# A running sum of gamma times v kept in SBUF, in place of a carry copied from tile to tile in PSUM

## The chip, the cores and the metric

The kernel runs on one core of one Trainium2 chip. The metric is the device time of one execution in microseconds. Before the change the median of three runs is 630.31 us (630.24 to 630.64).

## What is computed

The input x is 4 batches of 2048 tokens with 256 features, in float32. An attention layer without softmax is followed by a layer of softly routed experts; each is added to its input and normalised. The part that matters here is the attention:

```python
q, k, v = mlp_q(x), mlp_k(x), mlp_v(x)        # gelu(x @ W1 + b1) @ W2 + b2
scores = einsum('bid,bjd->bij', q, k) / scale
scores = scores * tril(ones((T, T)))          # causal, no softmax
out = einsum('bij,bjd->bid', scores, v)
out = layernorm(out) * ln_w + ln_b
x = layernorm(x + out)
```

There is no softmax, so the part of `out` that comes from earlier tiles is the product of a query with a running state (the sum of k transposed times v). The bias of q adds to each score a number that depends on the key token alone. The kernel calls it gamma: column 256 of `k_tok`. For a tile of 128 tokens, all earlier tiles therefore add two things: h of q times the state, and one row, the same for all 128 tokens, which is the sum of gamma times v over all earlier tokens.

## The kernel before the change, in words

64 tiles of 128 tokens stand in 16 groups of four; a batch is 16 tiles, four groups. Each engine runs its own program, a `body` for each group, called by `run_groups`. The body of group g projects group g (`project`) and attends for group a = g - 1 (`attend`); `ja` is the place of group a in its batch (0 to 3), i that of a tile in its batch (0 to 15) and c that of a tile in its group. Body 0 only projects. Body 15 (`more=False`) also begins the expert stage: it scales the first tokens and takes their norms. After it comes a last body that only attends, `last_chunks` on TensorE. The expert stage begins behind a barrier of all engines.

Products are made in three passes of a reduced type (`fp32r`): each operand is split into a rounded part (`_hi`, made by ScalarE) and a remainder (`_lo`, made by VectorE or GpSimd), and `split3` issues hi times hi, hi times lo and lo times hi.

TensorE's order in a body is: hidden layer of k (two jobs), scores of group a, hidden layer of q (two jobs), `chunk` 0, first job of v's hidden layer, `chunk` 1, second job of v's hidden layer, two tiles of k's projection, `chunk` 2, two more tiles of k's projection, `chunk` 3, first half of v's projection, transposes of k, second half of v's projection. A `chunk` holds, for one tile, the masked scores times v (`attend_chunk`, 3 matmuls), the queries times the state (`read_state`, 6), the update of the state in PSUM (`update_state`, 6), and the `carry` (3). The state is rounded by ScalarE (`round_state`) and split by VectorE (`split_state`) before the next tile reads it.

The row of gamma times v lives in the output tile in PSUM itself. `carry` of tile i adds gamma (broadcast over the 128 columns of the weights) times v of tile i into the output tile of i + 1, on top of the row that ScalarE had copied there from the output tile of i (`preload`, PSUM to PSUM). Gamma has its own rounding on ScalarE (in `round_ktok`) and its own split on VectorE (`split_gamma`). Two wide matmuls at the start (`mark_out`) set the output banks up, so that nothing later needs a starting matmul.

GpSimd's order in a body: `add_ln_b(g)` (adds ln_b to the loaded x), `split_hv(g, 0)`, `invert_o(a, 0)`, `split_hv(g, 1)`, `split_x(g + 1)`, `split_ktok(g, 0)`, `invert_o(a, 1)`, `split_ktok(g, 1)`, two `split_v`, `invert_z(a)`, `invert_x1(a)`. In body 15 `add_beta(0)` stands in place of `split_x`. VectorE's order: splits of k's hidden layer around `mask_scores`, `split_masked`, both splits of q's hidden layer, then `follow(0)` (the split of the state behind tile 0), statistics and outputs of tiles 0 and 1, biases of k and v, and at the end `split_gamma`, `z_statistics` and `z_deviation`. In body 15 `scale_tokens(0)` stands between the two splits of q's hidden layer and `scale_tokens(1)` behind `bias_k`. In body 0 VectorE ends with `mu_factors`, which waits for GpSimd's `invert_mu_norms`; TensorE's `spread_mu_factors` in body 1 waits for that.

The SP queue loads x transposed and x, one after the other, for each group: the first behind `x_split`, the second behind `xb_ready`, which `add_ln_b` signals.

## Time and profile before

| | before |
|---|---|
| median of 3 runs | 630.31 us |
| the profiled execution, its own time | 629.76 us |
| its span | 628.0 us |
| TensorE (PE) busy | 606.5 us, 97% |
| VectorE (DVE) busy | 432.7 us, 69% |
| ScalarE (ACT) busy | 414.8 us, 66% |
| GpSimd (POOL) busy | 349.8 us, 56% |
| mean granted clock of TensorE | 0.995 |

The span is what lies between the first and the last instruction; 1.76 us of the execution lie around it. The attention takes about the first 416 us, the expert stage the rest. Matmuls overlap, so the length shown for one (280 ns for 256 columns) is longer than the distance from its start to the next one's; a cost is read from the distance between starts.

### The profile page before, as it was taken

The page shows a single profiled execution, that of the slowest core. Times are in us where ns is not written, and L with a number is a line of the kernel's source. Part 1 is how long each engine was busy: PE and PEld are TensorE (multiplying, and loading weights), DVE is VectorE, ACT ScalarE, POOL GpSimd, SP SyncE. Part 2 cuts the span into 40 slices and gives each one's busy share as a digit, 9 for nine tenths or more (in the row PEclk, how much of TensorE's full clock was granted, in tenths as well). Part 3 has the DMA queues.
Part 4 walks back from the last instruction along what each step waited for, and adds up shares of the span by engine and source line. Part 5 has one row for each costly group of instructions (what it writes and reads, how often), then busy time and mean ns, then how long its engine had stood idle before and what let it go on. Part 6 is the DMA issues. An engine that isn't in the chain of part 4 may idle for free. (4 is left out here: it accounts for less than half of the span.)

```text
span 628.0 us, 12369 instructions
## 1 busy us (share of the span) xinstructions
PE 606.5 (97%) x4100; PEld 557.8 (89%) x4100; DVE 432.7 (69%) x943; ACT 414.8 (66%) x921; POOL 349.8 (56%) x359
## 2 busy tenths in 40 slices
PE   7999999999999999999999999999999999979994
PEld 5889999989999999899998998989999999868883
DVE  5587677677676776777767768886656554437784
ACT  4756767767677667676676776766766666334765
POOL 2937567676675675766766757665344333104443
PEclk9999999999999999999999999999999999999997
DMA  8311211111012012111120110030000000032444
GB/s 224 105 35 33 69 34 34 49 53 35 33 33 67 33 33 67 33 33 33 34 67 33 33 35 1 2 68 2 1 1 0 0 0 2 2 67 69 166 142 160
DMA packets 29310, 30.21 MB, mean 48 GB/s; under 512 B 5310, under 2 KB 25180, under 8 KB 29276
## 3 DMA queue, kind: packets, MB, share of 16 engines
q1 hardware_dynamic: 29264, 29.78, 15.9%
q8 instruction: 18, 0.29, 0.2%
q14 instruction: 16, 0.13, 0.1%
q10 hardware_dynamic: 12, 0.00, 0.0%
HBM read 21.39 MB, written 8.39 MB: 47 GB/s over the span
## 5 line engine op out<-in xcount | busy, mean ns | idle before, releaser
L563 ACT ACTIVATE h_hi<-bank,bias_col 128x512 fp32r<-128x512 f32 x96 | 66.4, 692 | 35.1 <-PE bank L690 31.7
L488 POOL TENSOR_TENSOR h_lo<-xn_all,h_hi 128x512 fp32r<-128x512 f32 x32 | 41.4, 1294 | 71.1 <-ACT xn_all L565 71.0
L688 PE MATMUL bank<-xnT_hi,w_hi 128*128 128x512 f32 x188 | 76.0, 404 | 0.0
L689 PE MATMUL bank<-xnT_lo,w_hi 128*128 128x512 f32 x188 | 74.2, 395 | 0.0
L690 PE MATMUL bank<-xnT_hi,w_lo 128*128 128x512 f32 x188 | 74.2, 395 | 0.0
L1067 DVE TENSOR_TENSOR state_lo<-bank,state_hi 128x512 fp32r<-128x512 f32 x57 | 39.1, 686 | 43.4 <-ACT state_hi L604 43.4
L1442 PE MATMUL bank<-xn_all,e_tok 128*128 128x257 f32 x256 | 66.4, 382 | 0.2
L1348 ACT ACTIVATE e_tok<-bank,shift,xinv 128x256 f32<-128x256 f32 x64 | 36.1, 565 | 44.9 <-PE bank L1425 24.0
L1522 DVE COPY ET_all<-bank 128x256 f32<-128x256 f32 (+1 forms) x64 | 27.0, 424 | 53.1 <-PE bank L1436 52.7
L494 POOL TENSOR_TENSOR ktok_lo<-xn_all,ktok_hi 128x512 fp32r<-128x512 f32 x32 | 38.1, 1192 | 44.3 <-ACT ktok_hi L580 44.3
L604 ACT CAST state_hi<-bank 128x512 fp32r<-128x512 f32 x57 | 33.5, 588 | 41.7 <-PE bank L830 41.5
L1514 PE MATMUL bank<-w_sb,ET_all 128*128 128x256 f32 x256 | 55.5, 379 | 0.8 <-ACT w_sb L1387 0.8
L1514 PEld LDWEIGHTS bank<-w_sb,ET_all 128*128 128x128 f32 x256 | 48.6, 190 | 7.6 <-ACT w_sb L1387 1.1
L483 POOL TENSOR_TENSOR x_all<-x_all,lnb_rows 128x512 f32 (+1 forms) x32 | 47.2, 1494 | 11.6 <-DMA x_all<-in_L_attn_x 11.6
L219 POOL TENSOR_TENSOR xn_all<-xn_all,b_rows 128x1024 f32<-128x1024 f32 x16 | 35.0, 2187 | 26.7 <-DVE xn_all L212 26.7
L1423 PE MATMUL bank<-mu_hi,xnT_hi 128*128 128x256 f32 x128 | 47.2, 369 | 0.8 <-POOL blank L1303 0.8
L1442 PEld LDWEIGHTS bank<-xn_all,e_tok 128*128 128x128 f32 x256 | 43.6, 190 | 4.3 <-ACT slot_inT L1370 0.9
L690 PEld LDWEIGHTS bank<-xnT_hi,w_lo 128*128 128x128 f32 x188 | 35.4, 188 | 8.6
L1011 DVE TENSOR_TENSOR h_lo<-hq,h_hi 128x512 fp32r<-128x512 f32 x32 | 32.4, 1016 | 13.9 <-ACT hq L565 13.9
L500 POOL TENSOR_TENSOR v_lo<-xn_all,v_hi 128x512 fp32r<-128x512 f32 x32 | 40.7, 1290 | 0.3 <-ACT v_hi L595 0.3
L689 PEld LDWEIGHTS bank<-xnT_lo,w_hi 128*128 128x128 f32 x188 | 35.5, 189 | 5.8
L688 PEld LDWEIGHTS bank<-xnT_hi,w_hi 128*128 128x128 f32 x188 | 35.4, 188 | 5.8
(188 smaller groups left out, 2072.0 us busy)
## 6 DMA issues: line engine op xcount, KB each, us to landing
x_all<-in_L_attn_x SPq DMA_DIRECT2D x16, 512.0 KB, 3.5
out<-xn_all SPq DMA_DIRECT2D x16, 512.0 KB, 3.0
xn_all<-in_xT SPq DMA_DIRECT2D x15, 512.0 KB, 3.7
w_sb<-in_L_ffn_w SPq DMA_DIRECT2D x2, 512.0 KB, 5.4
xn_all<-in_L_ffn_w SPq DMA_DIRECT2D x2, 512.0 KB, 6.3
xn_all<-in_xT SPq DMA_DIRECT2D x2, 256.0 KB, 3.6
x_all<-in_L_attn_W2k SPq DMA_DIRECT2D x1, 258.0 KB, 4.4
x_all<-in_L_attn_W2q SPq DMA_DIRECT2D x1, 258.0 KB, 5.4
```

The costliest lines, as they stand in the source:

```text
L483: pool.tensor_tensor(xp, xp, lnb_rows[:, :].unsqueeze(1).to_broadcast([P, 2, D]), ALU.add).then_inc(xb_ready, 1)
L488: pool.tensor_tensor(h_lo[:, V_SLOT, m, :], hv[:, m, :], h_hi[:, V_SLOT, m, :].bitcast(F32), ALU.subtract).then_inc(hv_split, 1)
L494: pool.tensor_tensor(ktok_lo[:, pair, :], k_tok[:, pair, 0:D], ktok_hi[:, pair, :].bitcast(F32), ALU.subtract).then_inc(ktok_split, 1)
L500: pool.tensor_tensor(v_lo[:, pair, :], v_tok[:, pair, :], v_hi[:, pair, :].bitcast(F32), ALU.subtract).then_inc(v_split, 1)
L563: nc.scalar.activation(h_hi[:, h_slot(j, n), m, :], ps, ACT.Gelu, bias=bias(n, m))
L688: nc.tensor.matmul(ps, w[0], xs[0], start=start, stop=False, skip_group_check=shared)
L689: nc.tensor.matmul(ps, w[0], xs[1], start=False, stop=False, skip_group_check=shared)
L690: return nc.tensor.matmul(ps, w[1], xs[0], start=False, stop=stop, skip_group_check=shared)
L1067: nc.vector.tensor_tensor(lo[:, :, :], state_halves, hi[:, :, :].bitcast(F32), ALU.subtract).then_inc(state_split, 1)
L1423: nc.tensor.matmul(ps, hi, mu_hi[:, kb, :], start=(kb == 0), stop=False)
L1442: last = nc.tensor.matmul(fold_ps[s][:, 0:D + 1], e_tok[:, t % 4, s * P:(s + 1) * P], xn[q][:, t % GT, :], start=(t == 0), stop=(t == TB - 1))
L1514: last = nc.tensor.matmul(mix_ps[k % 2][t][:, 0:D], ET_all[:, s, toks], so[:, k // GB, s, :], start=(s == 0), stop=(s == SB - 1))
```

## The change

- `carry` of tile c now adds the whole row at once: the 128 x 128 matrix of ones times a tile `v_sum`, whose row p is the sum over all earlier tiles of gamma times v at place p. It has two passes, ones times the rounded part and ones times the remainder. It stands inside `chunk`, behind the first of the two products, and the first product of a tile now starts the accumulation. Tile 0 of a batch has no carry.
- `v_sum` has four slots. VectorE fills them: `sum_v(c)` writes slot c + 1 from slot c, `close_sum` writes slot 0 for the next group. ScalarE rounds them in two pairs (`round_vsum`), GpSimd splits them in two pairs (`split_vsum`).
- The rounding and split of gamma, the copies `preload` and their waits are gone. Tiles 0 and 2 of a group now wait for `z_ready` on TensorE itself.
- VectorE: `follow(0)` stands ahead of the split of the second half of q's hidden layer.
- GpSimd: `add_ln_b(g)` goes from the head of the body to behind `split_x(g + 1)`; in body 15 it stands ahead of `add_beta(0)`.
- `causal` has one 128 x 128 block, not four.

```diff
 # GpSimd
-                pool.memset(causal[:, :, :], 1.0)
+                pool.memset(causal[:, :], 1.0)
...
+                def split_vsum(g, m):
+                    pool.wait_ge(vsum_rounded, 2 * g + m + 1)
+                    pair = slice(2 * m, 2 * m + 2)
+                    pool.tensor_tensor(vsum_lo[:, pair, :], v_sum[:, pair, :], vsum_hi[:, pair, :].bitcast(F32),
+                                       ALU.subtract).then_inc(vsum_split, 1)
...
+                    if attend and project:
+                        split_vsum(a, 0)
                     if project:
-                        add_ln_b(g)
                         split_hv(g, 0)
                     if attend:
                         invert_o(pool, a, 0)
                     if project:
+                        if attend:
+                            split_vsum(a, 1)
                         split_hv(g, 1)
                         if more:
                             split_x(g + 1)
-                        else:
+                        add_ln_b(g)
+                        if not more:
                             add_beta(pool, 0, 0)
                         split_ktok(g, 0)
...
                         split_v(g, 1)
+                        if not more:
+                            split_vsum(g, 0)
+                            split_vsum(g, 1)
                     if attend and project:
                         invert_z(pool, a, (j - 1) % 2)
 # ScalarE
-                    nc.scalar.copy(gam_hi[:, :], k_tok[:, :, D]).then_inc(gam_rounded, 1)
...
-                def preload(ba, i):
-                    act.wait_ge(carried, CB * ba + i - 1)
-                    act.wait_ge(z_ready, TB * ba + i + 2 - i % 2)
-                    nc.scalar.copy(out_tile(i % GT), out_tile((i - 1) % GT)).then_inc(preloaded, 1)
+                def round_vsum(g, m):
+                    act.wait_ge(v_summed, GT * g + 2 * m + 1)
+                    pair = slice(2 * m, 2 * m + 2)
+                    nc.scalar.copy(vsum_hi[:, pair, :], v_sum[:, pair, :]).then_inc(vsum_rounded, 1)
...
                     hidden(g, j, WK1, 0)
+                    if attend:
+                        round_vsum(a, 0)
                     hidden(g, j, WK1, 1)
...
                     if attend:
                         follow(0)
+                    if attend:
+                        round_vsum(a, 1)
                     hidden(g, j, WV1, 0)
...
                     round_v(g, 0)
                     if not more:
+                        round_vsum(g, 0)
                         norms(act, 0, 0, range(GT))
                     round_v(g, 1)
+                    if not more:
+                        round_vsum(g, 1)
 # TensorE
-                def carry(a, ba, i):
-                    c = i % GT
-                    if c == 0:
-                        pe.wait_ge(gam_split, a + 1)
-                    if i > 0:
-                        pe.wait_ge(preloaded, PB * ba + i)
-                    split3(out_tile((i + 1) % GT),
-                           (gam_hi[:, c:c + 1].to_broadcast([P, P]), gam_lo[:, c:c + 1].to_broadcast([P, P])),
-                           (v_hi[:, c, :], v_lo[:, c, :]), False, False, shared=True).then_inc(carried, 1)
+                def carry(a, c, start):
+                    pe.wait_ge(vsum_split, 2 * a + c // 2 + 1)
+                    if isinstance(a, int) and a == 0 and c == 1:
+                        pe.wait_ge(ones_rounded, 1)
+                    nc.tensor.matmul(out_tile(c), ones_r[:, :], vsum_hi[:, c, :], start=start, stop=False,
+                                     skip_group_check=True)
+                    nc.tensor.matmul(out_tile(c), ones_r[:, :], vsum_lo[:, c, :], start=False, stop=False,
+                                     skip_group_check=True)
 
                 def chunk(a, ja, ba, c, p):
                     i = GT * ja + c
-                    if 0 < i < TB - 1:
-                        pe.wait_ge(preloaded, PB * ba + i)
+                    if c % 2 == 0:
+                        pe.wait_ge(z_ready, GT * a + c + 2)
                     if i == 0:
-                        pe.wait_ge(z_ready, GT * a + 2)
                         last = attend_chunk(a, c, True, True)
                     elif c == 0:
-                        read_state(ba, i, c, p, False)
+                        read_state(ba, i, c, p, True, False)
+                        carry(a, c, False)
                         last = attend_chunk(a, c, False, True)
                     else:
-                        attend_chunk(a, c, False, False)
-                        last = read_state(ba, i, c, p, True)
+                        attend_chunk(a, c, True, False)
+                        carry(a, c, False)
+                        last = read_state(ba, i, c, p, False, True)
                     last.then_inc(chunk_done, 1)
                     if i < TB - 1:
                         update_state(a, c, i == 0)
-                        carry(a, ba, i)
...
                     def read(c):
-                        if c < GT - 1:
-                            pe.wait_ge(preloaded, PB * ba + i + c)
-                        read_state(ba, i + c, c, p, False, tail_hi[c], tail_lo[c])
+                        if c % 2 == 0:
+                            pe.wait_ge(z_ready, GT * a + c + 2)
+                        carry(a, c, c % 2 == 0)
+                        read_state(ba, i + c, c, p, False, False, tail_hi[c], tail_lo[c])
 # VectorE
+                def sum_v(g, j, c):
+                    dve.wait_ge(v_biased, 2 * g + c // 2 + 1)
+                    if not (isinstance(g, int) and g == 0):
+                        dve.wait_ge(v_summed, GT * g + c)
+                        dve.wait_ge(vsum_split, 2 * g)
+                    elif c > 0:
+                        dve.wait_ge(v_summed, c)
+                    gamma = k_tok[:, c, D:D + 1]
+                    if j == 0 and c == 0:
+                        last = nc.vector.tensor_scalar(v_sum[:, 1, :], v_tok[:, 0, :], gamma, None, ALU.mult)
+                    else:
+                        last = nc.vector.scalar_tensor_tensor(out=v_sum[:, c + 1, :], in0=v_tok[:, c, :], scalar=gamma,
+                                                              in1=v_sum[:, c, :], op0=ALU.mult, op1=ALU.add)
+                    last.then_inc(v_summed, 2 if j == GB - 1 and c == GT - 2 else 1)
+
+                def close_sum(g, j):
+                    if j < GB - 1:
+                        dve.wait_ge(v_summed, GT * g + GT - 1)
+                        dve.wait_ge(vsum_split, 2 * g + 1)
+                        nc.vector.scalar_tensor_tensor(out=v_sum[:, 0, :], in0=v_tok[:, GT - 1, :],
+                                                       scalar=k_tok[:, GT - 1, D:D + 1], in1=v_sum[:, GT - 1, :],
+                                                       op0=ALU.mult, op1=ALU.add).then_inc(v_summed, 1)
...
+                    if attend:
+                        sum_v(a, ja, 1)
+                        sum_v(a, ja, 2)
                     split_h(g, j, WQ1, 0)
                     if not attend:
                         split_m()
                     if not more:
                         scale_tokens(0, 0)
+                    if attend:
+                        follow(0)
+                        close_sum(a, ja)
                     split_h(g, j, WQ1, 1)
                     if attend:
-                        follow(0)
...
-                    split_gamma(g)
+                    sum_v(g, j, 0)
+                    if not more:
+                        sum_v(g, j, 1)
+                        sum_v(g, j, 2)
                     if attend:
                         z_statistics(a, p, 1)
...
                 split_first_x()
                 dve.wait_ge(masks_ready, 1)
+                nc.vector.tensor_copy(ones_r[:, :], ones[:, :]).then_inc(ones_rounded, 1)
                 spread_b2k()
```

## Rows read from the trace of the kernel before

**Rows 1.** Engines by stretch: length; busy us (instructions) by engine; TensorE's clock; DMA.

```profile
270.00:300.00 30.00, 30.00 (x222) 28.38 (x222) 20.66 (x42) 21.42 (x42) 19.39 (x19) 1.00 0.14 41
...
620.00:628.00 8.00, 0.00 (x0) 0.00 (x0) 1.03 (x3) 3.43 (x7) 1.13 (x2) 0.57 0.41 148
```

**Rows 2.** Waits of TensorE: us in total, times, longest.

```profile
PE bank L688 <- DVE state_lo L1067: 1.5, 4, 1.0
```

**Rows 3.** Groups of TensorE instructions: one of carry's three passes; busy us, mean ns.

```profile
L688 PE MATMUL bank<-v_hi,gam_hi 128*128 128x256 f32 x60 | 16.7, 279 | 0.0
```

**Rows 4.** Timeline, TensorE, a group with ja = 1: start us, length us.

```profile
152.69 0.39 PE L688 MATMUL bank<-xnT_hi,w_hi 128*128 128x512 f32 x1
...
160.81 0.28 PE L688 MATMUL bank<-v_hi,masked_hi 128*128 128x256 f32 x1
...
161.88 0.28 PE L688 MATMUL bank<-v_hi,gam_hi 128*128 128x256 f32 x1
...
162.23 0.40 PE L688 MATMUL bank<-xnT_hi,w_hi 128*128 128x512 f32 x1
```

**Rows 5.** Timeline, TensorE: tile 1's reads of the state that waited (ja = 0; body 15).

```profile
138.62 0.39 PE L688 MATMUL bank<-state_hi,h_hi 128*128 128x256 f32 x1 [0.17 <-DVE state_lo L1067]
...
390.22 0.38 PE L688 MATMUL bank<-state_hi,h_hi 128*128 128x256 f32 x1 [1.01 <-DVE state_lo L1067]
```

**Rows 6.** Groups by line: instructions with the shapes of the added ones.

```profile
L595 ACT CAST v_hi<-xn_all 128x512 fp32r<-128x512 f32 x32 | 19.9, 623 | 14.7 <-DVE xn_all L1047 14.7
L212 DVE SCALAR_TENSOR_TENSOR xn_all<-x_all,r_all,g_rows 128x256 f32<-128x256 f32 x64 | 26.6, 479 | 0.0
L500 POOL TENSOR_TENSOR v_lo<-xn_all,v_hi 128x512 fp32r<-128x512 f32 x32 | 40.7, 1290 | 0.3 <-ACT v_hi L595 0.3
```

**Rows 7.** Timeline, GpSimd: its part beside VectorE's instructions of rows 8.

```profile
127.86 2.58 POOL L500 TENSOR_TENSOR v_lo<-xn_all,v_hi 128x512 fp32r<-128x512 f32 x2
...
153.59 2.54 POOL L500 TENSOR_TENSOR v_lo<-xn_all,v_hi 128x512 fp32r<-128x512 f32 x2
...
158.32 1.01 POOL L204 TENSOR_TENSOR r_all<-ve_x,minus_half 128x4 f32 x1 [0.17 <-POOL ve_x L202]
159.29 3.00 POOL L483 TENSOR_TENSOR x_all<-x_all,lnb_rows 128x512 f32 x2
...
384.27 2.55 POOL L483 TENSOR_TENSOR x_all<-x_all,lnb_rows 128x512 f32<-128x512 f32 x2
```

**Rows 8.** Timeline, VectorE: instructions with two inputs in SBUF.

```profile
129.32 1.13 DVE L1040 TENSOR_TENSOR gam_lo<-xn_all,gam_hi 128x4 fp32r<-128x4 f32 x1
...
154.57 0.34 DVE L1040 TENSOR_TENSOR gam_lo<-xn_all,gam_hi 128x4 fp32r<-128x4 f32 x1
...
161.60 1.24 DVE L1011 TENSOR_TENSOR h_lo<-hq,h_hi 128x512 fp32r<-128x512 f32 x1 [0.46 <-ACT hq L565]
```

**Rows 9.** Timeline, GpSimd and TensorE, body 0 to body 1.

```profile
28.44 0.71 POOL L535 TENSOR_TENSOR mu_inv<-mu_n,minus_half 128x2 f32<-128x2 f32 x1
...
31.95 0.71 PE L916 MATMUL bank<-mu_diag,ones 128*128 128x128 f32 x4 [0.81 <-DVE mu_diag L1086]
```

**Rows 10.** Timeline, body 15 and the last body, all engines.

```profile
396.29 2.21 POOL L219 TENSOR_TENSOR xn_all<-xn_all,b_rows 128x1024 f32<-128x1024 f32 x1
...
399.42 1.67 DVE L212 SCALAR_TENSOR_TENSOR xn_all<-x_all,r_all,g_rows 128x256 f32<-128x256 f32 x4
...
404.43 0.42 ACT L226 ACTIVATE square<-xn_all 128x256 f32<-128x256 f32 x1
...
406.04 0.60 ACT L595 CAST v_hi<-xn_all 128x512 fp32r<-128x512 f32 x1
...
408.19 1.01 POOL L193 TENSOR_TENSOR r_z<-ve_z,minus_half 128x4 f32<-128x4 f32 x1 [0.18 <-DVE ve_z L175]
...
408.91 0.39 PE L830 MATMUL bank<-v_hi,ktok_hi 128*128 128x256 f32 x1 [0.16 <-DVE h_lo L1067]
...
415.33 0.28 PE L690 MATMUL bank<-v_hi,masked_lo 128*128 128x256 f32 x1
```

More of the change, by code:

```diff
@@ L283, in build @@
             ku_rows = asb("ku_rows", [P, KC])
-            gam_hi = asb("gam_hi", [P, GT], F32R)
-            gam_lo = asb("gam_lo", [P, GT], F32R)
+            v_sum = asb("v_sum", [P, GT, D])
+            vsum_hi = asb("vsum_hi", [P, GT, D], F32R)
+            vsum_lo = asb("vsum_lo", [P, GT, D], F32R)
+            ones_r = asb("ones_r", [P, P], F32R)
             bias_rows = asb("bias_rows", [3 * KB, P])
@@ L289, in build @@
             lnb_rows = asb("lnb_rows", [P, D])
-            causal = asb("causal", [P, GT, P])
+            causal = asb("causal", [P, P])
             xT_hi, xT_lo = xnT_hi[0], xnT_lo[0]
@@ L466, in _ @@
                                    base=0, pattern=[[-1, P]], channel_multiplier=1)
-                pool.affine_select(out=causal[:, :, :], in_=causal[:, :, :], compare_op=ALU.is_ge, fill=0.0,
-                                   base=0, pattern=[[0, GT], [1, P]], channel_multiplier=-1).then_inc(masks_ready, 1)
+                pool.affine_select(out=causal[:, :], in_=causal[:, :], compare_op=ALU.is_ge, fill=0.0,
+                                   base=0, pattern=[[1, P]], channel_multiplier=-1).then_inc(masks_ready, 1)
                 def split_x(g):
@@ L630, in body @@
                         round_masked(a)
-                        preload(ba, i + 3)
                         apply_z(act, a - 1, (ja - 1) % 2, (0, 1))
@@ L752, in fold_weights, with warm_up @@
                     last.then_inc(ku_done, 1)
-                def mark_out():
+                def warm_up():
                     for ps in out_ps:
-                        last = nc.tensor.matmul(ps[:, :], ident[:, :], causal[:, :, :].rearrange("p c n -> p (c n)"),
-                                                start=True, stop=True)
-                    last.then_inc(out_marked, 1)
+                        nc.tensor.matmul(ps[:, :], ident[:, :], causal[:, :].unsqueeze(1).to_broadcast([P, GT, P]),
+                                         start=True, stop=True)
                 def project_k(g, j, t):
@@ L804, in scores, with read_state @@
                         last.then_inc(scores_done, 1)
-                def read_state(ba, i, c, p, stop, hi=state_hi, lo=state_lo):
+                def read_state(ba, i, c, p, start, stop, hi=state_hi, lo=state_lo):
                     pe.wait_ge(state_split, CB * ba + i)
@@ L812, in read_state @@
                         last = split3(out_tile(c), (h_hi[:, p, kb, toks], h_lo[:, p, kb, toks]),
-                                      (hi[:, kb, :], lo[:, kb, :]), False, stop and kb == KB - 1, shared=True)
+                                      (hi[:, kb, :], lo[:, kb, :]), start and kb == 0, stop and kb == KB - 1, shared=True)
                     return last
```

23 lines of the change are left out of this document (7 added, 16 removed).

## The prediction

> **What bounds the kernel.** I read the engines by stretch first. In any full stretch of the attention TensorE is busy for all of it at clock 1.00, while VectorE has 69% and GpSimd 65% [rows 1]. Then TensorE's own waits: on another engine inside the attention's loop there is one entry, VectorE's split of the state, 1.5 us in four waits [rows 2]. So the loop is TensorE's, and matmuls taken out of it come off the time one for one, as long as nothing new ends late. The parts where TensorE isn't the bound are body 0 to body 1 and body 15 to the barrier; there chains over the other engines decide.
>
> **1. Fewer passes.** Before, 60 carries of three passes [rows 3]. Three passes take the step from 161.88 to 162.23 us, 0.35 us, so 0.117 us each [rows 4]. After, tiles 1 to 15 of each batch have two: 120. Outside `last_chunks` it is 171 against 112 (57 carries times 3; 56 times 2), 59 fewer: 59 x 0.117 = **-6.9 us**. That is all TensorE can give. I take no gain in `last_chunks`, which waits for other engines (5). The ScalarE copies `preload` go too; no wait of TensorE names them [rows 2], so they are worth nothing.
>
> **2. The state's split ahead of q's second.** Tile 1 reads the state behind VectorE. With ja = 0 that read began 0.17 us late by the row and about 0.32 by the distance of starts, and the next one 0.1 late: 0.42 us, in three batches. In body 15 it was 1.01 us late, some 1.27 in all, since `scale_tokens(0)` and q's second split (0.6 us) stood ahead [rows 5]. With ja = 0 the split now comes some 0.1 us before the need: -1.3. In body 15 I find 0.25 us of stall left (two `sum_v` are new ahead of it, q's second split is gone): -1.0. Together **-2.3 us** (-1.3 to -2.5).
>
> **3. The new wait: tile 0's carry.** With ja = 1, 2, 3 TensorE wants it right behind `read_state`, where the masked product stood: 8.12 us after the body's start (160.81 - 152.69) [rows 4]. Queued behind it are the whole body's matmuls. The chain that must be done: `sum_v(0)` on VectorE (0.48 us), `round_vsum(0)` on ScalarE (0.62), `split_vsum(0)` on GpSimd (1.29) [rows 6]. GpSimd gets to it only behind `invert_x1`, whose last instruction is followed by `add_ln_b` at 159.29 [rows 7]. ScalarE has been done for 3 us by then.
> What shifts 159.29? Rows 8 beside rows 7: VectorE's 4-column split of gamma took 1.13 us from 129.32 and ended when GpSimd's `split_v` did (130.44); from 154.57 it took 0.34 and ended about where the first `split_v` did. GpSimd in turn took 3.00 us for two `add_ln_b` with VectorE's 512-column split in between, 2.55 alone [rows 7, 8]. So an instruction of VectorE with two inputs in SBUF and one of GpSimd exclude each other, and 512 columns cost GpSimd 0.45 us. `sum_v(0)` has 256 columns and falls between the two `split_v`: +0.22. Then 159.51 + 1.29 + 0.05 = 160.85 against 160.81. It is a knife's edge; with a restart I take 0.1 us in each of 11 bodies (12 with ja > 0, less the last): **+1.1 us**. Bounds: 0, and 0.6 each, 6.6 us, if `sum_v(1)` (wanted at 159.88) gets in first.
> The Trainium skill, in "SBUF — State Buffer", section "SBUF: two separate sides", calls the pair shared by VectorE and GpSimd an exclusive lock held for the whole instruction, also against VectorE instructions with two SBUF inputs. Rows 7 and 8 agree for `tensor_tensor`; no row here has the form of `sum_v` against a long GpSimd instruction. Without the lock 3 would be 0 us and 5 would be 4.2 us.
>
> **4. Start and body 1.** The smaller `causal` lets TensorE start 0.6 us sooner, of which 0.4 is left behind the biases. But `add_ln_b(0)` (2.55 us) now stands ahead of `split_ktok(0)`, where GpSimd had no idle time; before, it came at the start and covered GpSimd's wait for h of v. So `mu_inv` (28.44) ends 2.1 us later even with the earlier start, and behind it `split_vsum` (1.29) starts at once, so `mu_factors` on VectorE is locked out until 32.6. `mu_diag` is ready at 33.2 and TensorE's product with it, which began at 31.95 after 0.81 us idle, begins at 33.2 [rows 9]: +1.3. VectorE is busy without a gap to tile 1's read and has two more `sum_v`: +0.3. **+1.6 us** (0 to 2.2).
> In the other bodies the moved `add_ln_b` falls in GpSimd's idle 3.2 us ahead of `split_ktok`, with 0.4 us to spare; if that went, `split_ktok` would be late by as much, and TensorE wants it 10 us later. Its DMA: x of the next group is queued some 13 us later and still has a body's 24 us until it is used; the next load of transposed x waits behind it by 3 us, with a body to spare. Nothing. `split_vsum(1)` fits in GpSimd's idle 1.4 us ahead of `split_hv(1)` and ends 0.25 us before tile 2's carry. `sum_v(1)`, `sum_v(2)` and `close_sum` fall in VectorE's idle time around q's splits. `z_ready` is a body old. Nothing each.
>
> **5. The end, body 15 and behind.** Here each edit hits a full engine [rows 10].
> - GpSimd: `add_ln_b(15)` (2.55 us) stands ahead of `add_beta(0)`, which moves from 396.3 to 398.9 and ends at 401.1. VectorE's `scale_tokens(1)` (two inputs in SBUF) wants to begin at 399.42 and is locked out: 1.7 us, and VectorE has no gap behind it. Perhaps `split_ktok` gets in between for another 1.2.
> - ScalarE: `round_vsum(15, 0)` stands ahead of the norms (404.43) and needs `sum_v(0)`, which VectorE reaches at the place of the old gamma split, 406.1, without the lock-out. So ScalarE stands idle, then does the norms (1.6 us), then `round_v(1)`, which began at 406.04: at 409.0 without lock-outs, 409.9 to 411.2 with them. Then a second `round_vsum` (0.52), the rounding of the turned tokens, the rounding of the state behind tile 12.
> - TensorE's update at 408.91 waits for that and comes at 412.5, 413.4 or 414.7.
> - GpSimd has two `split_vsum` (2.55) and the late `split_v` ahead of `invert_z` (408.19, then 414 to 415.6). VectorE's `shift_z` waits for it, and the next state split is queued behind `shift_z`.
> Followed on, the last matmul (415.33, and the barrier) comes 4.2 us later without the lock, 4.9 with it, 6.0 if `split_ktok` gets in. I take **+5.4 us** (3.4, ScalarE's chain alone, to 6.5).
>
> **Sum.** -6.9 - 2.3 + 1.1 + 1.6 + 5.4 = **-1.1 us**. It is made against the profiled execution (629.76 us: span 628.0 and 1.76 around it), 0.55 us below the median; the change goes on the median: 630.31 - 1.1 = **629.2 us**. A difference under 0.2% (1.3 us) can't be told from none here, so the forecast lies just inside "the same".
>
> **Rivals.**
> - A, the ends are covered. If ScalarE's and GpSimd's queues at the end bend less (5 at its low bound, 3.4), body 1 costs nothing and the first carry is never late, the sum is -6.9 - 2.3 + 3.4 = -5.8: **624.5 us**. For it: 5 is a chain of ten steps, each a place to be wrong. Against: `round_vsum(15, 0)` ahead of the norms waits for the end of VectorE's queue whatever else happens.
> - B, slower: tile 0's carry waits 0.5 us in each of the 11 bodies, since `sum_v(1)` or a later `invert_x1` pushes `split_vsum(0)` out. 4.4 us more than forecast, **633.6 us**. It decides from a lateness of 0.2 us more: at 0.3 us a body (3.3 us in place of 1.1) the kernel is slower. For it: the margin is -0.04 us. Against: the lateness doesn't add up, since a TensorE that waits gives the chain its time back.
> - C, the clock. Where TensorE did nothing for the 8 us of the last stretch, the granted clock was 0.57 [rows 1], so it was at the lower level (1.2 GHz) for most of it. The end now has a stall of some 4 us. If the clock falls there, the 4.6 us of matmuls behind it take up to twice as long, part of it hidden by their waits: +2.3, **631.5 us**. Against: before, no stretch inside the attention is below 1.00.
> The Trainium skill, "TensorE: Matmul & The Clock Gate", section "What's actually happening", says that idleness takes the clock to the lower level and activity gives it back. Last stretch and loop agree with both levels; no row of before has a stall of 4 us inside the work.
>
> **How the numbers follow.** Forecast 0.50, A 0.22, B 0.16, C 0.12. The forecast's own range is 627.4 to 630.9. Faster by over 0.2% (under 629.05): A's 0.22 and 0.21 of the forecast, 0.43. Within 0.2%: 0.26 of the forecast, 0.02 of B, 0.06 of C, 0.34. Slower: 0.03, 0.14 and 0.06, 0.23. Range 625.8 to 632.2: past the forecast's own on both sides, with most of C, half of A and the near part of B; the rest is under 2 in 10.
>
> **What would show it.** (1) Two passes a carry, 120 in all, 0.117 us apart. (2) No wait of TensorE on the state's split with ja = 0, at most 0.3 us in body 15. (3) TensorE waits on GpSimd's `vsum_lo`, about 11 times, 0 to 0.2 us; GpSimd's `split_vsum(0)` ends within 0.2 us of the carry's start. `sum_v(0)` begins when a `split_v` ends. (4) TensorE's product with `mu_diag` begins near 33.2 us with over 2 us idle. (5) ScalarE idle some 3 us ahead of the norms in body 15, TensorE's second update in `last_chunks` some 4 to 6 us after where it stood, counted from the end of v's projection, and the barrier 4.9 to 6 later. I am wrong if the barrier moves by under 3 us, if the carry waits over 0.3 us a body, or if the expert stage, which has no edit, takes another time.

## The result and the profile after

The changed kernel takes 635.28 us (median, 634.27 to 635.80) against 630.41 for the kernel before beside it: ratio 1.0075, 95% interval 1.0058 to 1.0093. Measured again later it is 1.0070 (1.0055 to 1.0086). By these ratios it is slower by 4.4 to 4.7 us; forecast was 1.1 us faster, and the range ended at 632.2. Even the fastest of its ten executions, 632.74 us, lies above that.

The first profiled execution took 635.80 us (span 634.1; before 629.76 and 628.0). I set TensorE's marks side by side: the first transposition of k in each body, the first matmul of the expert stage, and the last.

| stretch | before | after | difference | forecast |
|---|---|---|---|---|
| start to k's turn in body 0 | 22.73 | 24.41 | +1.7 | -0.4 |
| body 1 | 27.77 | 29.85 | +2.1 | +1.3 |
| bodies 2 to 14 | 324.99 | 320.62 | -4.4 | -6.0 |
| body 15 | 26.51 | 25.98 | -0.5 | -1.4 |
| k's turn in body 15 to the experts | 14.45 | 21.40 | +7.0 | +5.4 |
| expert stage | 202.00 | 202.31 | +0.3 | 0 |

(Forecast: the terms of the prediction laid on these stretches; body 1 is 2.0 less six passes.) The loop gave less than thought, and both ends took more. First the carry, groups of TensorE's instructions, answering to [rows 3]: busy, mean ns, idle time ahead.

```profile
L852 PE MATMUL bank<-vsum_hi,ones_r 128*128 128x256 f32 x60 | 17.5, 291 | 0.1
L854 PE MATMUL bank<-vsum_lo,ones_r 128*128 128x256 f32 x60 | 17.1, 285 | 0.0
```

There are 120 passes, and TensorE's idle time ahead of the carries is 0.1 us in all. GpSimd's `split_vsum(0)` and TensorE's carry in a group with ja = 1 (timeline) show how near it is:

```profile
161.78 1.30 POOL L506 TENSOR_TENSOR vsum_lo<-v_sum,vsum_hi 128x512 fp32r<-128x512 f32 x1
...
163.19 0.32 PE L852 MATMUL bank<-vsum_hi,ones_r 128*128 128x256 f32 x1
163.35 0.28 PE L854 MATMUL bank<-vsum_lo,ones_r 128*128 128x256 f32 x1
```

The split ends 0.1 us ahead of the use; the prediction had it 0.04 us behind. Next TensorE's waits, answering to [rows 2]:

```profile
PE bank L843 <- DVE h_lo L1099: 4.3, 1, 4.3
...
PE bank L927 <- DVE mu_diag L1118: 2.3, 1, 2.3
...
PE bank L244 <- DVE xn_all L1054: 1.2, 1, 1.2
...
PE bank L715 <- ACT bias_col L632: 0.7, 1, 0.7
```

The waits for `state_lo` are gone from the top of this list (one of 0.4 us is left, in body 15); four waits at the two ends stand there. Engines by stretch; the number behind POOL's is TensorE's granted clock, which was 1.00 in the same stretches before:

```profile
35.00:38.00 3.00, 2.89 (x9) 2.50 (x10) 2.93 (x9) 0.59 (x1) 0.00 (x0) 0.50 0.00 0
...
411.00:413.00 2.00, 0.00 (x0) 0.00 (x0) 1.56 (x2) 1.98 (x4) 2.00 (x3) 1.00 0.00 0
414.00:417.00 3.00, 3.00 (x16) 3.00 (x16) 2.26 (x7) 2.06 (x4) 3.00 (x3) 0.50 0.00 0
```

Behind the 2.27 us without work in body 1, and behind the 4.34 us in `last_chunks`, the clock stands at its lower level, 1.2 GHz: 9 matmuls in 3 us of body 1, 20 in the same stretch before. The first hidden matmuls are slow too (timeline, TensorE, the last line from the kernel before):

```profile
6.02 0.27 PE L911 MATMUL bank<-ident,bias_rows 6*128 6x6 f32 x1
7.02 2.07 PE L715 MATMUL bank<-xnT_hi,w_hi 128*128 128x512 f32 x4 [0.73 <-ACT bias_col L632]
8.89 1.91 PE L719 MATMUL bank<-xnT_hi,w_lo 128*128 128x512 f32 x4
```

```profile
8.22 1.10 PE L705 MATMUL bank<-xnT_hi,w_lo 128*128 128x512 f32 x4
```

Four took 1.91 us, 1.10 before. This is not a fall of the clock but a late rise. The trace's first record of the clock, at the full level, begins at some 11.1 us of the span here and at some 6.7 us in the trace of before. Ahead of it there is no record (the view then prints 1.00), and the rate of the matmuls is what shows the lower level; it goes up where that record begins.

Body 1, answering to [rows 9] (timelines of three engines):

```profile
32.56 0.71 POOL L548 TENSOR_TENSOR mu_inv<-mu_n,minus_half 128x2 f32<-128x2 f32 x1
33.25 1.26 POOL L506 TENSOR_TENSOR vsum_lo<-v_sum,vsum_hi 128x512 fp32r<-128x512 f32 x1
...
33.31 1.22 DVE L1114 TENSOR_SCALAR mu_fac<-mu_inv,scale_col 128x2 f32<-128x2 f32 x1 [4.32 <-POOL mu_inv L548]
...
35.11 1.22 PE L927 MATMUL bank<-mu_diag,ones 128*128 128x128 f32 x4 [2.27 <-DVE mu_diag L1118]
```

`mu_fac` begins 0.06 us behind `split_vsum` and ends with it. The end, answering to [rows 10]:

```profile
397.82 2.20 POOL L219 TENSOR_TENSOR xn_all<-xn_all,b_rows 128x1024 f32<-128x1024 f32 x1
...
398.64 3.79 DVE L212 SCALAR_TENSOR_TENSOR xn_all<-x_all,r_all,g_rows 128x256 f32<-128x256 f32 x4
...
400.82 1.33 POOL L494 TENSOR_TENSOR ktok_lo<-xn_all,ktok_hi 128x512 fp32r<-128x512 f32 x1 [0.79 <-ACT ktok_hi L592]
...
407.33 0.62 ACT L601 CAST vsum_hi<-v_sum 128x512 fp32r<-128x512 f32 x1 [2.24 <-DVE v_sum L1071]
407.85 0.41 ACT L226 ACTIVATE square<-xn_all 128x256 f32<-128x256 f32 x1
...
409.46 0.60 ACT L606 CAST v_hi<-xn_all 128x512 fp32r<-128x512 f32 x1
...
413.30 0.39 PE L843 MATMUL bank<-v_hi,ktok_hi 128*128 128x256 f32 x1 [4.34 <-DVE h_lo L1099]
...
421.45 0.28 PE L704 MATMUL bank<-v_hi,masked_lo 128*128 128x256 f32 x1
```

This is the forecast chain, link by link: `scale_tokens(1)` locked out, `split_ktok` in between, ScalarE idle ahead of the norms, then `round_v(1)` and TensorE's update. The forecast's times are on the clock of the kernel before, where k's turn in body 15 came 1.1 us later (402.00, here 400.86). Brought to that clock `round_v(1)` is at 410.6 (forecast 409.9 to 411.2 with lock-outs) and the update at 414.4 (412.5 to 414.7). What the forecast leaves out is the matmuls behind.

The expert stage, which has no edit, takes 0.3 us more; that was one of the prediction's signs of being wrong. In this profile the clock falls there too, for 3.4 us from 557.2, and in that of before it doesn't. But in the trace of `before_state_first` it falls there as well, and that stage is within 0.1 us of before's. So the clock doesn't explain it, and the cause stays open.

### The profile page after: what moved, and what is told of

Same layout as the page of the kernel before. It is cut to its first block and busy times, and to the rows that moved or that the text cites. A ratio compares the mean times of both kernels' runs of the same rounds, so it can differ in the third digit from the quotient of the medians.

```text
span 634.1 us, 12270 instructions
## 1 busy us (share of the span) xinstructions
PE 608.6 (96%) x4040; PEld 559.4 (88%) x4040; DVE 449.0 (71%) x989; ACT 412.8 (65%) x881; POOL 384.9 (61%) x391
## 5 line engine op out<-in xcount | busy, mean ns | idle before, releaser
L500 POOL TENSOR_TENSOR v_lo<-xn_all,v_hi 128x512 fp32r<-128x512 f32 x32 | 42.8, 1362 | 3.1 <-ACT v_hi L606 3.1
L236 POOL TENSOR_TENSOR xinv<-n_low,minus_half 128x4 f32<-128x4 f32 x16 | 16.3, 1016 | 42.6 <-DVE n_low L231 42.6
L506 POOL TENSOR_TENSOR vsum_lo<-v_sum,vsum_hi 128x512 fp32r<-128x512 f32 x32 | 41.2, 1289 | 0.0
```

Of the source, the lines that this page charges most:

```text
L500: pool.tensor_tensor(v_lo[:, pair, :], v_tok[:, pair, :], v_hi[:, pair, :].bitcast(F32), ALU.subtract).then_inc(v_split, 1)
L506: pool.tensor_tensor(vsum_lo[:, pair, :], v_sum[:, pair, :], vsum_hi[:, pair, :].bitcast(F32), ALU.subtract).then_inc(vsum_split, 1)
```

## The experiments

Differences in us are (ratio - 1) x 630.3.

**The addresses.** In the loop the matmuls of the projections followed each other more slowly than before, though nothing in them was changed. The changed kernel's larger tensors move h and all behind it by 11,232 bytes.

```diff
             gam_lo = asb("gam_lo", [P, GT], F32R)
+            pad = asb("pad", [P, 2808])
```

> The kernel before with one unused tensor of 11,232 bytes per partition ahead of h_hi, so that h_hi, h_lo, v_hi, ktok_hi, state_hi and all behind them lie at the addresses that they have in the changed kernel; no instruction differs. Question: in the changed kernel the matmuls of the projections follow each other more slowly than before (the time from m_hi by h_hi to m_lo by h_hi 126 ns against 118, from w_lo by h_hi to w_hi by h_lo 120 against 117), some 0.14 us a body, about 2 us in all. Theory ADDRESS: it is the place of these tensors in SBUF; this kernel then takes 632.4 us (631.5 to 633), and its trace has the spacings of the changed kernel. Rival TRAFFIC: it is the other engines' new work on SBUF (sum_v, round_vsum, split_vsum) beside the matmuls; then this kernel is the kernel before, 630.4 us within 0.3, with spacings of 118 and 117. Chances 0.6 and 0.4.

Ratio 1.0025 (1.0016 to 1.0034): +1.6 us with not one instruction changed. Groups of TensorE in 75 to 375 us, first of the kernel before, then of this one:

```profile
L690 PE MATMUL bank<-w_hi,h_lo 128*128 128x256 f32 x97 | 27.0, 279 | 0.0
L688 PE MATMUL bank<-m_hi,h_hi 128*128 128x258 f32 x96 | 27.0, 281 | 0.0
```

```profile
L689 PE MATMUL bank<-m_hi,h_hi 128*128 128x258 f32 x96 | 27.2, 284 | 0.0
...
L691 PE MATMUL bank<-w_hi,h_lo 128*128 128x256 f32 x96 | 27.0, 282 | 0.0
```

These two groups take 3 ns more each. Of the six groups on `h_hi` and `h_lo` in this stretch five are longer, by 1 to 4 ns, and one (`m_hi,h_lo`) is not; those on the state are not longer. Marks of bodies 2 to 14 (first transposition of k), before:

```profile
50.50 1.04 PE L788 MATMUL bank<-ident,xn_all 128*128 128x128 f32 x8
...
375.49 1.04 PE L788 MATMUL bank<-ident,xn_all 128*128 128x128 f32 x8
```

and with the padding:

```profile
51.20 1.04 PE L789 MATMUL bank<-ident,xn_all 128*128 128x128 f32 x8
...
377.56 1.04 PE L789 MATMUL bank<-ident,xn_all 128*128 128x128 f32 x8
```

326.36 against 324.99: +1.4 us of these 13 bodies. The theory ADDRESS holds, with a little less than the 2 us that it expected; the traffic of the other engines isn't needed for most of it.

```diff
             ones_r = asb("ones_r", [P, P], F32R)
+            pad = asb("pad", [P, 8])
```

> The changed kernel with one unused tensor of 32 bytes per partition ahead of bias_rows, so that h_hi and all behind it lie 11,264 bytes (11 times 1,024) behind where they lay before, in place of 11,232. Theory ADDRESS with an alignment of up to 1,024 bytes: the spacings of the projections go back to 118 and 117 ns, some 2 us less, 633.3 us (632.5 to 634.2). ADDRESS without a role of this alignment, or TRAFFIC: 635.3 us within 0.8. The stalls and the clock at the start, in body 1 and at the end are not touched.

Ratio 1.0081 (1.0063 to 1.0098), no gain; bodies 2 to 14 take 320.42 us (320.62). A distance of 11 times 1,024 bytes doesn't restore the pace, so alignment of up to 1,024 isn't what decides.

```diff
-            v_sum = asb("v_sum", [P, GT, D])
-            vsum_hi = asb("vsum_hi", [P, GT, D], F32R)
-            vsum_lo = asb("vsum_lo", [P, GT, D], F32R)
             ones_r = asb("ones_r", [P, P], F32R)
+            ones = asb("ones", [P, P])
+            b1_row = asb("b1_row", [PAIRS, P])
+            pad = asb("pad", [P, 8])
...
             b2_row = asb("b2_row", [E, D])
+            v_sum = asb("v_sum", [P, GT, D])
+            vsum_hi = asb("vsum_hi", [P, GT, D], F32R)
+            vsum_lo = asb("vsum_lo", [P, GT, D], F32R)
```

> The changed kernel with v_sum, vsum_hi and vsum_lo laid behind all other tensors of the attention, and ones, b1_row and 32 unused bytes in the gap, so that h_hi, h_lo and all up to mu_diag lie at the addresses of the kernel before; no instruction differs. The kernel before with these tensors at the changed kernel's addresses took 1.6 us more. Theory ADDRESS ALONE: the changed kernel gets back what the other lost, 1.6 us, ratio to before 1.0050, and w_lo by h_hi to w_hi by h_lo takes 117 ns again (120). Theory ADDRESS AND TRAFFIC: half of it, 0.5 to 1.0 us. Rival: any new place costs, since other tensors now meet each other: under 0.4 us. Chances 0.5, 0.25, 0.25.

Ratio 1.0051 (1.0033 to 1.0068), 1.2 to 1.5 us under the two measurements of the changed kernel, though the intervals overlap; bodies 2 to 14 take 319.51 us, 1.1 less. So most comes back. Which pair of tensors meets where stays open.

**The start.**

```diff
                                         ).then_inc(bias_turned, 1)
+                    nc.tensor.matmul(out_ps[0][:, 0:3 * P], ident[:, :],
+                                     causal[:, :].unsqueeze(1).to_broadcast([P, 3, P]), start=True, stop=True)
```

> The changed kernel with one more matmul of 384 columns on ident and causal behind the transposition of the biases, into a bank that is overwritten later; it fills the 0.73 us in which TensorE had nothing to do from 6.29 to 7.02 us. Theory CLOCK AT THE START: the changed kernel's first hidden matmuls ran at half rate (4.72 us for twelve of 512 columns, 2.91 before) because TensorE was idle just behind the warm-up; with the gap filled they take 2.9 to 3.3 us, the fold begins at 10.0 to 10.4 us (11.74 without, 10.09 before), and the whole is 1.4 us shorter: 633.9 us. Rival: it is the earlier begin of the warm-up (2.31 us, 2.99 before) that counts, and the clock rises no sooner whatever fills the gap: 635.3 us or 0.1 more, the fold at 11.7. A second rival: the two kernels' rates at the start differ from one execution to the next, and one profile doesn't tell; then the time moves by under 0.5 us. Chances 0.5, 0.25, 0.25.

Ratio 1.0073 (1.0060 to 1.0086): no gain in the median, though in its profile the first four hidden matmuls take 1.39 us and the fold (the matmuls on `x_all` behind them) begins at 10.05 us, as forecast by the first theory. The second rival has to be taken too. Of eight profiles of the changed kernel and its edits without the filling, five have the half rate: the fold begins at 11.3 to 12.1 us, and the first record of the full clock at some 10.6 to 11.9. Three have not (fold at 9.4 to 10.6, record at 5.4 to 6.8). The warm-up begins at 2.31 us in all eight. TensorE's idle time behind it is 0.3 to 0.9 us in the five and 0.6 to 1.4 us in the three, so neither the earlier begin nor the length of the gap decides by itself. Both profiles with the filling have the full rate (record at 6.3 and 6.8), and so have the four of the kernel before and its edits (6.2 to 8.5; in the padded one it comes within the first hidden matmuls). Where the rate is full, k's turn in body 0 comes at 22.5 to 23.3 us with the change, by and large where it was (22.73); where it is half, at 24.0 to 24.8: +1.7 us in the first profile. That the filling prevents it is suggested by two profiles and not shown by the times.

**Body 1.**

```diff
                     if project:
+                        if not attend:
+                            add_ln_b(g)
                         split_hv(g, 0)
...
-                        add_ln_b(g)
+                        if attend:
+                            add_ln_b(g)
```

> The changed kernel with add_ln_b(0), and it alone, back at the head of GpSimd's body 0. My step 4: mu_inv (32.56 us in the changed kernel) comes some 2.5 us sooner, near 30.1, since GpSimd covers its wait for h of v again; mu_fac is no longer locked out by split_vsum; TensorE's product with mu_diag, which began at 35.11 after 2.27 us without work, begins near 33.4 with 0.3 to 0.9 us without. Theory STALL AND CLOCK: with a stall that short the granted clock stays 1.00 in 34 to 38 us (0.50 for 3.4 us of it in the changed kernel, price some 1.7 us), so the gain is 1.5 + 1.6 = 3.1 us: 632.2 us (631.5 to 633). Rival STALL ALONE (the clock falls all the same, or it fell in the profiled execution alone): 1.5 us, 633.8 us. Rival: the stall has another cause (VectorE's sum_v in body 1): under 0.5 us.

Ratio 1.0032 (1.0021 to 1.0043): 2.4 to 2.7 us less, outside the intervals of the changed kernel. Timelines of GpSimd and VectorE, and the stretch of the clock row:

```profile
30.48 0.71 POOL L551 TENSOR_TENSOR mu_inv<-mu_n,minus_half 128x2 f32<-128x2 f32 x1
31.94 1.28 POOL L506 TENSOR_TENSOR vsum_lo<-v_sum,vsum_hi 128x512 fp32r<-128x512 f32 x1 [0.74 <-ACT vsum_hi L604]
```

```profile
31.23 0.23 DVE L1117 TENSOR_SCALAR mu_fac<-mu_inv,scale_col 128x2 f32<-128x2 f32 x1 [0.69 <-POOL mu_inv L551]
```

```profile
35.00:38.00 3.00, 3.00 (x18) 2.42 (x17) 2.80 (x5) 2.77 (x6) 0.00 (x0) 1.00 0.00 0
```

Without GpSimd beside it `mu_fac` takes 0.23 us, not 1.22; TensorE doesn't wait there, and the clock stays. Body 1 takes 26.35 us: 3.5 less than with the change, 1.4 less than before it. My price for the fall (1.7) was too high: two profiles (of end_queues and third_pass below) have the same 2.27 us stall and no fall, and their body 1 is 0.8 to 1.0 us shorter (29.03, and 29.25 less three added passes of 0.117, against 29.85); that the waits behind take in the rest is likely and not shown.

**The moves alone, on the kernel before.**

```diff
                     if attend:
                         follow(0)
+                    split_h(g, j, WQ1, 1)
```

(VectorE; `split_h` stood ahead of `follow(0)`.)

> The kernel before with one edit of the change alone: VectorE splits the state behind tile 0 ahead of q's second split. My step 2: TensorE's waits for that split (1.5 us in four) and the launches behind them, 0.42 us in each of three batches and 1.0 in body 15, go: 2.3 us less, ratio 0.9964. Rival: q's second split, 0.6 us later, now lets tile 1 or the scores of the next group wait; then the gain is under 1 us. Rival: in body 15 the gain is given back where v_hi is waited for: 1.3 us.

Ratio 0.9969 (0.9957 to 0.9981): -2.0 us, forecast -2.3. Bodies 2 to 14 give 1.25 us (forecast 1.3), body 15 0.6 (1.0): the read there still waits 0.41 us.

```diff
                     if project:
-                        add_ln_b(g)
                         split_hv(g, 0)
...
                             split_x(g + 1)
+                        add_ln_b(g)
```

> The kernel before with one edit of the change alone: GpSimd's add_ln_b behind the splits of h of v and of x, in every body. Body 1: mu_inv would come some 2.5 us later (28.44 to 30.9), but with add_ln_b(1) gone from behind it mu_fac is not locked out (1.23 us before) and no split_vsum stands there, so TensorE's product with mu_diag comes near 31.9 as before: 0 us (0 to 0.8). Body 15: add_ln_b(15) and add_beta(0) lie on scale_tokens(1), which takes 3.8 us in place of 1.67; v's biases, and all behind them, come 1.2 us later at TensorE: 1.2 to 2.1 us. Sum 1.5 us, ratio 1.0024. Theory that the move costs by itself what the whole change loses in body 1 (3 us with the clock): ratio 1.006 or more. Rival, it costs nothing alone: ratio 1.0000 within 0.0008.

Ratio 0.9981 (0.9971 to 0.9991): -1.2 us where I expected +1.5. The missed effect: `add_ln_b` at the head of a body locked VectorE's `split_h` of q out (1.24 us in [rows 8], 0.69 in this run), and the state's split behind it came late for that. With it moved, the waits go in the loop (1.25 us, the same ones as in the run above, so the two don't add) and body 15 is 1.2 us shorter. The price at the end is 0.6 us, not 1.2 to 2.1, with `scale_tokens(1)` at

```profile
397.52 3.03 DVE L212 SCALAR_TENSOR_TENSOR xn_all<-x_all,r_all,g_rows 128x256 f32<-128x256 f32 x4
```

and body 1 loses 0.5 us (1.30 us stall at `mu_diag`, 0.81 before, no fall of the clock).

**The end.** First the order of two queues:

```diff
                     if not more:
-                        round_vsum(g, 0)
                         norms(act, 0, 0, range(GT))
                     round_v(g, 1)
                     if not more:
+                        round_vsum(g, 0)
                         round_vsum(g, 1)
...
                         split_v(g, 1)
-                        if not more:
-                            split_vsum(g, 0)
-                            split_vsum(g, 1)
                     if attend and project:
                         invert_z(pool, a, (j - 1) % 2)
+                        if not more:
+                            split_vsum(g, 0)
+                            split_vsum(g, 1)
```

> The changed kernel with two orders altered in body 15: on ScalarE the norms and round_v(1) come ahead of both round_vsum(15); on GpSimd invert_z comes ahead of both split_vsum(15). My step 5, ScalarE's share: without the wait for sum_v(0) (2.24 us idle) the norms begin at 404.9 and round_v(1) at 406.6 in place of 409.46; then the rounding of the second vsum waits for sum_v(2) at 408.6, so the turned tokens are rounded at 409.1 (410.49) and TensorE's second update of last_chunks comes near 411.3 in place of 413.30. The gain is 2.0 us if the clock falls all the same in the stall of 2.3 us that is left, 3.7 if it doesn't: 633.3 or 631.6 us, ratio to before 1.0043 or 1.0016. Rival: GpSimd and VectorE are the bound there, and the barrier moves by under 1 us.

Ratio 1.0055 (1.0039 to 1.0070), and not from the end: from k's turn in body 15 to the experts it takes 21.49 us (21.40); this profile has no fall in body 1. ScalarE, VectorE, TensorE (timelines):

```profile
408.76 0.62 ACT L601 CAST vsum_hi<-v_sum 128x512 fp32r<-128x512 f32 x1 [1.62 <-DVE v_sum L1071]
```

```profile
405.88 2.16 DVE L1071 SCALAR_TENSOR_TENSOR v_sum<-xn_all,v_sum 128x256 f32<-128x256 f32 x2
```

```profile
411.62 0.58 PE L843 MATMUL bank<-v_hi,ktok_hi 128*128 128x256 f32 x1 [3.47 <-DVE h_lo L1099]
```

`round_v(1)` comes early, and GpSimd's `split_v(1)` with it, which now locks out `sum_v` (2.16 us for two, 1.18 in the change). ScalarE waits for the last `sum_v` in place of the first. The stall is 3.47 us and the clock falls behind it again.

```diff
                     if project:
+                        if not more:
+                            add_ln_b(g)
                         split_hv(g, 0)
```

> The same, and add_ln_b(15) back ahead of split_hv(15, 0), so that add_beta(0) and split_ktok no longer lie on scale_tokens(1). My step 5, the lock-out's share: scale_tokens(1) takes 1.67 us in place of 3.79, v's biases and the turning of the tokens come 1.2 us sooner (TensorE's idle 1.16 us ahead of it goes), and the end gains 1.2 to 2.1 us over the run before it: ratio to before 1.0005 to 1.0025. Rival: the last body's own chain (state splits behind each other on VectorE, two more split_vsum on GpSimd) hides it; under 0.5 us.

Ratio 1.0081 (1.0049 to 1.0113): no gain, and the interval overlaps with that of the run before it. The end is shorter, 18.68 us in place of 21.49, but body 15 is 2.2 us longer (28.23 against 25.99). `add_ln_b(15)`, behind `split_vsum` now, lies on q's split (1.78 us, 0.69 in the run before it). The scaling of tokens comes later for that and runs beside `split_hv` (2.70 us in place of 1.67), and the state's split stands behind it. Waits of TensorE:

```profile
PE bank L846 <- DVE h_lo L1102: 3.4, 1, 3.4
PE bank L705 <- DVE state_lo L1102: 3.0, 1, 3.0
```

Neither order helped. So the next edit takes the work out of these queues.

```diff
-                        carry(a, c, c % 2 == 0)
+                        nc.tensor.matmul(out_tile(c), ones_r[:, :], vsum_hi[:, 0, :], start=c % 2 == 0, stop=False,
...
+                        nc.tensor.matmul(out_tile(c), ones_r[:, :], vsum_lo[:, 0, :], start=False, stop=False,
...
+                        for d in range(c):
+                            split3(out_tile(c), (gam_hi[:, d:d + 1].to_broadcast([P, P]),
+                                                 gam_lo[:, d:d + 1].to_broadcast([P, P])),
+                                   (v_hi[:, d, :], v_lo[:, d, :]), False, False, shared=True)
```

That is `read(c)` of `last_chunks`. In body 15 the rounding and the split of gamma stand in place of `sum_v`, `round_vsum` and `split_vsum` of the group; only `v_sum[:, 0]` is rounded and split. `add_ln_b(15)` goes behind the last `invert_x1`. The old addresses, the filling and `add_ln_b(0)` first are in it too.

> The changed kernel up to group 14, with the old addresses, the gap at the start filled and add_ln_b(0) first; for group 15 no v_sum is built beyond the one that group 14 leaves: the tiles of last_chunks take that in by two passes with ones each, and the group's own earlier tiles by three passes with gamma as before the change (26 carry passes there, 9 before, 8 in the change); add_ln_b(15) is the last work of GpSimd in the attention. If my steps are right the end costs 17 passes of 0.117 us, 2.0 us, over the kernel before, and neither ScalarE nor GpSimd is late: loop -4.4 - 1.5, state's split in body 15 -1.0, body 1 and start -0.5, end +2.0: 624.9 us, ratio 0.992 (0.990 to 0.995). Rival: the end has a cause that I don't see and keeps its +6 us: ratio 0.9985. Rival: the clock falls there all the same since the last body is one of waits: ratio 0.995 to 0.998.

624.42 us (624.24 to 624.70), ratio 0.9910 (0.9896 to 0.9924), forecast 0.992. It beats both kernels: 5.6 us under the kernel before. That the sum came so near is in part luck: start and body 1 gained 0.9 us more than forecast, and body 15 and the end cost 1.1 us more. TensorE's update, the last work of GpSimd, the clock:

```profile
401.54 0.39 PE L855 MATMUL bank<-v_hi,ktok_hi 128*128 128x256 f32 x1 [0.51 <-DVE h_lo L1123]
```

```profile
406.45 2.72 POOL L487 TENSOR_TENSOR x_all<-x_all,lnb_rows 128x512 f32<-128x512 f32 x2
```

```profile
399.00:403.00 4.00, 3.30 (x26) 3.14 (x27) 3.29 (x11) 3.06 (x6) 3.83 (x5) 1.00 0.00 0
403.00:408.00 5.00, 5.00 (x44) 5.00 (x44) 4.34 (x7) 3.20 (x7) 4.76 (x7) 1.00 0.01 3
```

The stall is 0.51 us in place of 4.34, and the end takes 17.12 us, 2.7 over before (forecast 2.0 for 17 more passes), 4.3 under the change. Bodies 2 to 14 take 318.92 us. The edit takes out the group's sums, their rounding and splits, and moves `add_ln_b(15)`, all at once; which of them gives how much isn't separated.

**The price of a pass, and the kernel again.**

```diff
+                    for _ in range(2):
                         nc.tensor.matmul(out_tile(c), ones_r[:, :], vsum_lo[:, c, :], start=False, stop=False,
```

> The changed kernel with the second pass of each carry issued twice (so vsum_lo counts twice in the sum): 60 passes more, 56 of them where TensorE has no idle time and 4 in last_chunks. My step 1 has 0.117 us for one: 6.6 us and up to 0.5 more, ratio 1.018. It tells whether the removed passes were worth 6.9 us. Rival, passes are partly hidden behind other waits (carry 0, the state's splits): 3 to 5 us, ratio 1.012 to 1.0155.

Ratio 1.0166 (1.0153 to 1.0179), 5.7 to 6.0 us over the change, between forecast and rival. In bodies 2 to 14 it is 325.88 - 320.62 = 5.3 us for 49 passes, 0.107 us each, 0.117 by the row.

> The changed kernel itself once more, so that the edits of it are set against one of the same call, and for a second profile. Ratio 1.0075 as measured. TensorE's clock: if the fall in body 1 (34.9 to 38.4 us) and in last_chunks (413.8 to 417.2) belong to the kernel, both are there again within some us; if the half rate of the first hidden matmuls belongs to one execution only, it may be gone.

Ratio 1.0070. All three disturbances are there again: the half rate at the start, a 2.27 us stall with the clock's fall in body 1, 4.34 us with its fall in `last_chunks`; the marks agree with the first profile within 0.2 us.

## Why the prediction was wrong

1. **Fewer passes, -6.9 us: right in kind, a little too large.** By 0.107 us a pass 59 are 6.3 us.
2. **State's split, -2.3: right** (2.0 alone). But the moved `add_ln_b` removes the same waits by itself, and I had priced that move at nothing in the loop.
3. **Tile 0's carry, +1.1: too large.** 0.1 us in all. The order was right, but the split ends 0.1 us ahead where I had 0.04 us behind; rival B is out.
4. **Start and body 1, +1.6.** The chain is right link by link (`mu_inv` late, `mu_fac` locked out, over 2 us idle); the product came at 35.1, not 33.2, of which 1.7 is the start. Without the fall of the clock body 1 costs 1.1 to 1.3 us over before, forecast 1.3. What I left out is TensorE's clock: 1.7 us at the start, where it rose late, and 0.8 to 1.0 behind the stall, where it fell. I asked at the end alone whether it might fall, and I had a forecast of over 2 us idle in body 1 on the table.
5. **The end, +5.4: right up to the stall**, then too small. The update comes 5.5 us later behind k's turn (12.44 against 6.91; forecast 3.6 to 5.8); from it to the experts takes 8.96 us in place of 7.54, +1.4. That this is the clock the rows below the list show. So rival C is there, at 1.4 us in the first profile and 2.3 (what I had for it) in another with the same stall. That the group-15 work is what costs, together with the place of `add_ln_b(15)`, is shown by the hybrid.
6. **Not in the list at all: the new tensors move the old ones**, 1.4 us in bodies 2 to 14 by the padded kernel. I took the loop's other matmuls as unchanged.

That the 1.4 us of point 5 are the clock is shown by four profiles of the same stretch with more and less of it at the lower level (the changed kernel, `after_gap_filled`, `after_old_addresses` and, with two queues in another order, `after_end_queues`; the number behind POOL's is the clock):

```profile
413.30:422.26 8.96, 8.43 (x57) 8.26 (x57) 6.11 (x15) 3.87 (x9) 6.47 (x16) 0.81 0.00 0
```

```profile
411.82:421.29 9.47, 8.94 (x56) 8.76 (x57) 6.11 (x15) 3.87 (x9) 6.49 (x16) 0.76 0.00 0
```

```profile
411.06:420.86 9.80, 9.27 (x56) 9.09 (x57) 6.11 (x15) 3.88 (x9) 6.49 (x16) 0.73 0.00 0
```

```profile
411.62:421.54 9.92, 9.39 (x57) 9.22 (x57) 6.53 (x15) 4.36 (x9) 6.48 (x16) 0.72 0.00 0
```

The clock's means make 3.4, 4.5, 5.3 and 5.6 us at the lower level. The stretch grows by some 0.45 us with each; taken down to none by that slope it is 7.4 us, an estimate, and 7.54 was measured before.

The step that failed is the clock: the sum has no term for it, and rival C had 0.12, for the end alone, on the ground that "before, no stretch inside the attention is below 1.00". But the kernel before had no stall inside the attention longer than 1.01 us, so its rows couldn't tell what 2.27 and 4.34 us would do. What the runs showed in its place is a fall behind both stalls, 0.9 and 1.4 us, and a late rise at the start, 1.7 us: 4.0 of the 7.2 us by which the table misses the forecast. The late rise is in part luck of the execution, since three profiles of the same edits don't have it. The addresses, a term that I put at nothing, are 1.4 more. The other 1.8 us are a balance: a pass is worth less (+0.6), the carry costs less (-1.0), the expert stage takes 0.3 more, and some 1.9 us no run takes apart, 0.9 of them in body 15 (of which the wait of 0.39 us was foreseen as 0.25).

The lock of the pair VectorE and GpSimd, which the Trainium skill states in "SBUF — State Buffer", section "SBUF: two separate sides", held for `sum_v`'s form too: 0.48 us alone, 2.16 us for two beside `split_v`. The Trainium skill's "TensorE: Matmul & The Clock Gate", section "What's actually happening", says that idleness takes the clock down; the traces agree, but the same 2.27 us took it down in six profiles and not in two.

## What to carry to other kernels

A stall of a tuned TensorE has two prices, its length and the matmuls behind it at half rate. Whether the second falls due differs from one execution to the next: here none of the four stalls of 0.7 to 1.3 us in body 1 took the clock down, six of eight of 2.27 us did, and all nine of 3.4 to 4.4 us at the end. Charge it at every stall of some 2 us and more; here it was 0.8 to 2.3 us each. Work taken off the bound engine must not land in the first and last body of a pipeline, where the other engines' queues are full; give the last group its old form. And a tensor that is added moves the ones behind it: run the old kernel with the padding alone before explaining a few ns a matmul by anything else.

## What I had not expected of the hardware

The same instructions at other addresses in SBUF: up to 4 ns more for matmuls of 256 and 258 columns on the projections' tensors (279 to 282, 281 to 284 in the groups shown), 1.6 us of the whole. A shift of 11,232 bytes did it; with 11,264 the pace was no better. And the start: in five profiles of eight the clock rose only at 10.6 to 11.9 us, though the warm-up had begun at 2.31, and in the other three at 5.4 to 6.8 us.
